# Where the inverse roots of a layer norm are taken, and how many signals TensorE gives per pair

## The reference, cut to what matters

```python
proj = gat_out @ Wp + bp
h = x + jax.nn.elu(proj)
mu = jnp.mean(h, axis=-1, keepdims=True)
var = jnp.mean((h - mu) ** 2, axis=-1, keepdims=True)
out = (h - mu) * jax.lax.rsqrt(var + LN_EPS) * gamma + beta      # first inverse root
...
x = _layernorm(x + out, axis=-1)                                 # second inverse root
```

## Time and profile before

| | us |
|---|---|
| median of three runs | 1848.58 (1843.01 to 1853.82) |
| the profiled execution | 1859.29 |
| its span, first to last instruction | 1857.5 |
| mean granted clock of TensorE | 0.805 |
| TensorE, VectorE, ScalarE, GpSimd busy | 69%, 65%, 47%, 54% |

### The profile page before, as it was taken

The page is one execution under the profiler, slowest core; times in us unless marked ns, Lnnn a source line. Parts: engine busy times, 40 slices in busy tenths (PEclk is TensorE's granted clock), DMA queues, the critical chain, the costliest instruction groups (busy, mean ns, idle before and its releaser), DMA issues. The chain is left out here.

```text
span 1857.5 us, 19719 instructions
## 1 busy us (share of the span) xinstructions
PE 1280.9 (69%) x5229; PEld 791.0 (43%) x5253; DVE 1202.5 (65%) x2284; ACT 876.8 (47%) x1944; POOL 994.5 (54%) x993
## 2 busy tenths in 40 slices
PE   5887787787787782068888887427667666666662
PEld 4555555555555551023444444314343344333331
DVE  4767667667667676857776777318475566665574
ACT  2667667657666673034444443405343344443341
POOL 5655555555555530003555555555676666776665
PEclk9898898888899896579888888558777777777776
DMA  4445545555545542011111111113122222222310
GB/s 114 138 149 170 156 142 169 160 152 163 165 142 162 163 135 95 0 28 30 44 51 46 44 43 44 27 38 69 36 67 50 59 61 62 61 61 50 74 46 22
DMA packets 162058, 161.98 MB, mean 87 GB/s; under 512 B 82994, under 2 KB 99681, under 8 KB 161948
## 3 DMA queue, kind: packets, MB, share of 16 engines
q1 hardware_dynamic: 130300, 130.80, 22.8%
q0 software_dynamic: 31648, 29.92, 7.7%
HBM read 66.88 MB, written 83.27 MB: 81 GB/s over the span
## 5 line engine op out<-in xcount | busy, mean ns | idle before, releaser
L277 POOL DMA_INDIRECT ids_pairs<-in_x_dram,gix x392 | 383.7, 979 | 296.9 <-PE bank L605 149.5
L1208 POOL DMA_INDIRECT x_table<-first_xr,first_rows x200 | 202.3, 1011 | 331.8 <-DVE first_xr L1445 273.3
L1605 POOL DMA_INDIRECT second_raw<-x_table,gix x196 | 201.0, 1026 | 142.7 <-PE twin L1711 60.8
L1611 POOL DMA_INDIRECT out_dram<-second_orow,last_rows x196 | 202.5, 1033 | 70.8 <-issue 58.5
L587 PE MATMUL twin<-AC,dense_hb 128*128 128x256 f32 x784 | 198.1, 397 | 37.7 <-DVE dense_hb L741 25.5
L579 PE MATMUL bank<-dense_xT,Mblk 128*128 128x512 f32 x196 | 125.6, 727 | 71.5 <-ACT dense_rl L670 53.2
L587 PEld LDWEIGHTS twin<-AC,dense_hb 128*128 128x128 f32 x784 | 147.0, 198 | 64.9 <-DVE dense_hb L741 31.4
L749 DVE TENSOR_REDUCE dense_v<-dense_q 128x8 f32<-128x512 f32 x98 | 66.7, 681 | 110.7 <-ACT dense_q L645 108.9
L1245 PE MATMUL twin<-first_zb,Mhead 128*128 128x512 f32 x200 | 129.3, 736 | 0.0
L595 PE MATMUL bank<-prm,dense_xT 128*128 128x128 f32 x784 | 118.5, 300 | 2.4 <-DVE dense_yc L784 2.3
L1385 DVE TENSOR_TENSOR first_zb<-twin,first_df 128x512 f32<-128x512 f32 x100 | 66.6, 686 | 79.0 <-remote 58.8
(11 more groups left out here) (360 smaller groups left out, 3072.5 us busy)
## 6 DMA issues: line engine op xcount, KB each, us to landing
x_table<-dense_yc SPq DMA_DIRECT2D x98, 260.0 KB
ids_rows<-in_x_dram SPq DMA_DIRECT2D x98, 256.0 KB
out_dram<-dense_orow SPq DMA_DIRECT2D x98, 256.0 KB
XT<-dense_turned SPq DMA_DIRECT2D x50, 256.0 KB
target_rows<-first_xr SPq DMA_DIRECT2D x50, 128.0 KB
ids_pairs<-in_x_dram,gix POOLq DMA_INDIRECT x392
second_targets<-target_rows SPq DMA_DIRECT2D x49, 128.0 KB
first_mask<-mask_rows SPq DMA_DIRECT2D x50, 64.0 KB
```

Source lines behind the costliest of these rows:

```text
L277: pool.indirect_dma_start(out=pairs[e % 2][:, j % 4, F * (j // 4):F * (j // 4) + F], out_offset=None, in_=x, in_offset=bass.IndirectOffset ...
L1208: pool.indirect_dma_start(out=x1, out_offset=bass.IndirectOffsetOnAxis(ap=first_rows[:, at + j:at + j + 1], axis=0), in_=xr[b][:, 2 * j + ...
L1605: pool.indirect_dma_start(out=raw[u.off % 3][:, 2 * j + s, :], out_offset=None, in_=x1, in_offset=bass.IndirectOffsetOnAxis(ap=gix[:, at:a ...
L1611: pool.indirect_dma_start(out=out, out_offset=bass.IndirectOffsetOnAxis(ap=last_rows[:, at:at + 1], axis=0), in_=orow[u.off % 4][:, 2 * j ...
```

## The change: what it does

ScalarE's `guess_roots` goes. VectorE adds eps itself (`add_eps` for the first variance, one more instruction in `sum_squares` for the second) and calls `root_step` eight times per slot for pairs u-2 and u-3 together, with `elu` after step 3 and `residual` after step 6. `refine_roots` goes, the roots are positive, and `flag` moves from between `scale` and `add_scaled` of pair u-4 to the end of the slot for pair u-3. TensorE signals `z_used` and `rows_made` only with the last instruction: 1 + 1 in place of 5 + 4, so 9 signals per pair; the waits on them follow. `centre` waits for `add_eps` of the pair before (`v1_made`) in place of ScalarE's guess. At the start `v` and `start` are cleared, and ScalarE's load of its table at the head of the stage goes.

```diff
@@ TensorE
-                    nc.tensor.matmul(pY[b][:, :], Mhead[:, n - 1, :] if n else Mblk[:, :], zb[n][:, :],
-                                     start=(n == 0), stop=(n == H)).then_inc(z_used, 1)
+                    last = nc.tensor.matmul(pY[b][:, :], Mhead[:, n - 1, :] if n else Mblk[:, :], zb[n][:, :],
+                                            start=(n == 0), stop=(n == H))
+                    if n == H:
+                        last.then_inc(z_used, 1)
...
                 def centre(u):
                     pe.wait_ge(h_made, u.count(1))
-                    atleast(pe, root_steps, 4 * u.count(0))
+                    atleast(pe, v1_made, u.count(0))
...
-                    nc.tensor.matmul(pC[:, c], xd[u.off % 4][:, c], Cm, start=True, stop=True).then_inc(rows_made, 1)
+                    last = nc.tensor.matmul(pC[:, c], xd[u.off % 4][:, c], Cm, start=True, stop=True)
+                    if j == 3:
+                        last.then_inc(rows_made, 1)
@@ ScalarE
-                act.add_instruction(mybir.InstLoadActFuncSet(
-                    name=nc.get_next_instruction_name(), engine=mybir.EngineType.Activation, act_func_set_id=EXP_AND_LN))
...
-                def guess_roots(u):
...
-                    if u.back(2).valid(PAIRS + 1):
-                        guess_roots(u.back(2))
@@ VectorE
                 def own_part(u):
...
-                    atleast(dve, z_used, u.count(-1) * (H + 1) + 1)
+                    atleast(dve, z_used, u.count(0))
...
                 def product(u, h):
                     dve.wait_ge(spread_made, u.count(0) * H + (h + 1))
-                    atleast(dve, z_used, u.count(-1) * (H + 1) + (h + 2))
...
+                def add_eps(u):
+                    dve.wait_ge(var_made, u.count(1))
+                    atleast(dve, roots_made, u.count(0))
+                    nc.vector.tensor_scalar(v[:, 0:8], pR[:, 0:8], EPS, None, ALU.add).then_inc(v1_made, 1)
+
                 def sum_squares(u):
                     dve.wait_ge(squared, u.count(1))
-                    atleast(dve, root_steps, 4 * u.count(1))
+                    atleast(dve, v2_made, u.count(0))
                     nc.vector.tensor_reduce(s2[:, :], q2[:, :, :], AX.X, ALU.add).then_inc(s_made, 1)
-
-                def refine_roots(u):
...
+                    dve.wait_ge(s_made, u.count(1))
+                    dve.wait_ge(roots_made, u.count(1))
+                    nc.vector.tensor_scalar(v[:, 8:16], s2[:, :], EPS, None, ALU.add).then_inc(v2_made, 1)
+
+                def root(u, k):
+                    if k == 1:
+                        if u.valid(PAIRS):
+                            dve.wait_ge(v1_made, u.count(1))
+                        atleast(dve, v2_made, u.count(0))
+                    if k == ROOT_STEPS:
+                        atleast(dve, flagged, u.count(-1))
+                        atleast(dve, scaled, u.count(0))
+                    root_step(nc, dve, k, v[:, :], w[:, :], ta[:, :], tb[:, :], root_steps, u.count(0), roots_made)
...
-                                            ALU.subtract).then_inc(yc_made, 1)
+                                            ALU.add).then_inc(yc_made, 1)
...
-                    if u.back(3).valid(PAIRS + 1):
-                        refine_roots(u.back(3))
...
-                    if u.back(4).valid(PAIRS):
-                        flag(u.back(4))
...
-                    if u.back(1).valid(PAIRS):
-                        elu(u.back(1))
-                        residual(u.back(1))
+                    if u.back(2).valid(PAIRS):
+                        add_eps(u.back(2))
+                    for k in range(1, ROOT_STEPS + 1):
+                        if has_roots:
+                            root(u.back(2), k)
+                        if k == 3 and u.back(1).valid(PAIRS):
+                            elu(u.back(1))
+                        if k == 6 and u.back(1).valid(PAIRS):
+                            residual(u.back(1))
+                    if u.back(3).valid(PAIRS):
+                        flag(u.back(3))
```

More of the change, by code:

```diff
@@ L1141, in gnn @@
             s2 = sbp("s2", [128, 8])
-            ve, ln, guess, halved, off, w = (sbp(n, [128, 16]) for n in ("ve", "ln", "guess", "halved", "off", "w"))
+            v, w, ta, tb = (sbp(n, [128, 16]) for n in ("v", "w", "ta", "tb"))
             wf = sbp("wf", [128, 8])
@@ L1149, in gnn @@
             stored = [semp(f"stored{i}") for i in range(4)]
[L1150 to L1154, removed]
+            (spread_made, z_made, z_used, diff_made, crossed, scanned, xd_copied,
+             e_made, g_made, h_made, hc_made, sq_made, var_made, rows_made, v1_made, roots_made, root_steps, scaled,
+             yc_made, squared, s_made, v2_made, xr_made, cleared, flagged) = (semp(n) for n in (
+                 "spread_made", "z_made", "z_used", "diff_made", "crossed", "scanned",
+                 "xd_copied", "e_made", "g_made", "h_made", "hc_made", "sq_made", "var_made", "rows_made",
+                 "v1_made", "roots_made", "root_steps", "scaled", "yc_made", "squared", "s_made", "v2_made", "xr_made",
+                 "cleared", "flagged"))
             block = ph.enter_context(nc.Block())
@@ L1305, in _ @@
             def _(act):
-                act.add_instruction(mybir.InstLoadActFuncSet(
-                    name=nc.get_next_instruction_name(), engine=mybir.EngineType.Activation, act_func_set_id=EXP_AND_LN))
                 def copy_targets(u):
-                    atleast(act, rows_made, u.count(-3) * 4)
+                    atleast(act, rows_made, u.count(-3))
                     nc.scalar.activation(xd[u.off % 4][0:64, :], XT[64:128, columns(u, 0)], ACT.Identity,
@@ L1327, in square @@
                     act.wait_ge(hc_made, u.count(1))
-                    atleast(act, rows_made, u.count(0) * 4)
+                    atleast(act, rows_made, u.count(0))
                     nc.scalar.activation(sq[:, :], pH[:, :], ACT.Square, bias=ncbeta[:, :])
@@ L1388, in scan @@
                     b, half = u.off % 2, slice(64 * s, 64 * s + 64)
-                    dve.wait_ge(z_used, u.count(1) * (H + 1))
+                    dve.wait_ge(z_used, u.count(1))
                     atleast(dve, e_made, u.count(-1))
                     atleast(dve, crossed, u.count(0) * 2 + (1 - s))
-                    nc.vector.tensor_tensor_scan(ys[b][half, ::-1], mask[b][half, ::-1], pY[b][half, ::-1],
-                                                 start[half, :] if u.count(0) or not s else 0.0,
+                    nc.vector.tensor_tensor_scan(ys[b][half, ::-1], mask[b][half, ::-1], pY[b][half, ::-1], start[half, :],
                                                  ALU.mult, ALU.add).then_inc(scanned, 1)
@@ L1457, in slot @@
                     if u.static() and u.count(0) == 0:
+                        nc.vector.memset(v[:, :], 1.0)
                         for b in range(4):
                             nc.vector.memset(xr[b][:, :, F:F + 1], 1.0)
+                        nc.vector.memset(start[:, :], 0.0).then_inc(cleared, 1)
+                        dve.wait_ge(cleared, 1)
+                    has_roots = u.back(2).valid(PAIRS + 1)
                     if u.valid(PAIRS):
```

10 lines of the change are left out of this document (1 added, 9 removed).

## The result

The changed kernel takes 1795.72 us (four runs, 1792.19 to 1799.92), the kernel before took 1845.80 us beside it (four runs, 1836.99 to 1853.82): ratio 0.9724 [0.9687, 0.9760] (in brackets here and below: the 95% interval), 50.1 us less. On other chips the same change makes the kernel 1.3% slower; that is what the experiments are about.

A forecast was written before the change was run, and what follows sets the result against it. VectorE was taken as the bound (10.51 us of an 11.03 us slot), late TensorE signals stretching the mean to 13.95. Pairs 42 us less, 3 us more behind: -39 from 1859.29 gives 1820, median 10.7 lower: 1810 us, range 1797 to 1826.

The forecast's parts named there:

- The steps on VectorE: Small instructions in each slot of stage first: net 1.40 us more work, bounds 0.7 to 2.3, undisturbed slot 11.9 us.
- Nothing covers this: VectorE's added steps lie behind the second scan, where the load hides all but 0.52 us, so they are paid.
- The long waits go: Forecast case, chance 0.43: in the pairs TensorE's late signals mostly stop holding VectorE; 24 slots of 11.9 us, 49 us less.
- Both go the right way: GpSimd's idle between batches becomes 1.7 us and signals per batch fall from 16 to 9, both against late signals.
- The pairs as 24 like slots with an allowance: Pairs of stage first: 24 slots at 12.2 us, with 0.3 us each for slightly late signals, 293 us, 42 us less.
- Behind the last pair: Slots after the last pair: VectorE makes two or three more rounds of 1.4 us, 3 us more.
- the load of the table: ScalarE's load at the head of the stage goes: at most 1 us, at the start.
- Shorter waits, same balance: Rival, 0.26: GpSimd's idle share drains signals, so slots settle at 13.0 to 13.9 us; -22 to 0 us, middle 1836 us.
- The waits stay and VectorE pays: slower: Rival, 0.31: long waits remain in the pairs and VectorE's added steps are paid; +21 us, 1870 us, or 1881 us.
- 10 free slots: In the slower rival (0.31), pairs' slots without long waits or their aftermath pay the added 1.4 us in full: 14 us.
- Signals by the rule: Serialized increments at 26.3 ns: 7 signals fewer give back 0.18 us per pair, 4.6 us in all; not in the forecast sum.

The follow-up runs named there:

- before9: The kernel before with 9 signals of TensorE per pair in place of 16: 1557.23 us, 1.0004 on chip 3; 1854.04 us, 1.0053 on chip 7.
- filler7: The kernel before with seven useless dependent steps of VectorE per slot, 16 signals kept: 1742.47 us, 0.9716 on chip 9; 1575.19 us, 1.0087 on chip 1.
- after16: The changed kernel with 16 signals of TensorE per pair in place of 9: 1754.43 us, 0.9768 on chip 13; 1581.81 us, 1.0160 on chip 3.
- filler4: The kernel before with four useless dependent steps of VectorE per slot, 16 signals kept: 1792.17 us, 0.9975 on chip 13.
- half_scatter: The kernel before without four of the eight scatters of each pair, rows left unwritten: 1752.07 us on chip 7, 1548.71 us on chip 3, one run each.

## Why the prediction was right in its mechanism and short in its size

The direction held, and so did the main line of the mechanism: the long waits go and VectorE pays for its steps. What failed is the size of two terms of the sum, the pairs (293 us forecast, 286.9 us measured) and the stretch behind them (3 us more forecast, 1.7 us less measured). The forecast was 1810 us; 1795.72 us lies 14.3 us under it and 1.3 us under the low end of the range. That low end was drawn in: 24 slots at 0.7 us in place of 1.40 give 1793 us, which the measured time would have met, and redone from the bounds of 0.12 and 0.30 us for ten steps the net is about 0.6 to 2.4 us and not 0.7 to 2.3.

- **The steps on VectorE: right, a little low.** Forecast 1.40 us more work and a slot of 11.9 us, measured 1.55 and 12.06; L147, at 0.34 us where an instruction of 0.17 was taken, is as large as the difference. "Nothing covers this" was right for a slot that runs undisturbed, beyond the 0.52 us that the forecast took off. The net cost against such a slot, 11.9 - 11.03 = 0.87 us, came out at 1.02 us on the quiet chip 3; that 20.8 us over 24 slots is 0.87 us too is chance, since the first four slots paid nothing.
- **The long waits go: right, but for one.** The forecast's sign in the trace was no wait of VectorE for "remote" over 3 us and `own_part` 25 times within 285 to 300 us. It is 1.1 us at most and 286.9 us. ScalarE kept one wait of 10.7 us.
- **What heals them: half right.** "Both go the right way" named the pause and the number of signals. before9 on chip 7 (1.0053 with all waits in place) rules the signals out; filler7 on chip 9 (0.9716) and after16 on chip 13 (0.9768) leave the pause.
- **The pairs as 24 like slots with an allowance: failed, 5.9 us too high.** "I allow 0.3 us per slot for signals that are a little late" made 24 x 12.2 = 293 us. The slots took 286.9 us. The fifth `own_part` of the kernel after splits them:

```profile
846.15 0.69 DVE L1365 SCALAR_TENSOR_TENSOR first_zb<-first_mask,first_xd 128x512 f32<-128x512 bf16 x1
```

  The first four slots, in which the pipeline fills, took 40.0 us, where four at 12.2 are 48.8. They took 40.0 us in the kernel before as well, and the forecast priced them as full ones. The other twenty took 247.0 us, where twenty at 12.2 are 244: the usual slot is 12.06 us and not 11.9, and the one long wait that was left made two of them 14.5 and 14.6 us long, about 5 us together. So the signals that are late did cost something like the 7.2 us allowed for them, in one piece. That 286.9 us is also 24 x 11.9 to within 1 us, the sum without an allowance, is luck: short first slots against longer steps and one wait.
- **Behind the last pair: wrong sign, 4.7 us.** "3 us more" became 1.7 us less. As the price of the added rounds the 3 us were right: on quiet chips that stretch takes 74.5 us in before9 and 77.7 to 78.0 us in after16 and the changed kernel. On the late chip it takes 85.5 us before and 83.8 us after, so some 11 us of lateness stood in it before and some 6 us after. The long waits in it, first before, then after:

```profile
ACT first_ve L1343 <- remote: 10.6, 1, 10.6
```

```profile
ACT XT L1077 <- remote: 8.0, 1, 8.0
```

  I had read the waits only up to the last pair, and so priced the late stretch as if it were undisturbed.
- The two terms make 10.6 us. The stretch up to the first pair took 1.1 us more, where it was to lose the load of the table (1.28 us in the trace of before, at L1306, and not "at most 1 us"). 2.8 us more come from the medians: the forecast started from 1848.58 us, and the runs beside the result gave 1845.80. The 2 us that are left lie between profiled executions and medians, and in rounding.
- **"Shorter waits, same balance" (0.26):** the waits didn't settle at a shorter length. In filler4 on chip 13 they keep their seven times and up to 9.6 us, and in filler7 they are nearly gone. What lies between looks like an edge and not a balance, as far as two points on two chips show. That the rival put its finger on GpSimd was right: half the scatters, no waits. Its own form, that GpSimd's share of the slot decides and not the pause, isn't excluded: a batch of 10.2 us fills 91% of filler4's slot of 11.16 us and 87% of filler7's slot of 11.79 us.
- **"The waits stay and VectorE pays: slower" (0.31):** this is what the change does on a quiet chip, 1.0131 [1.0111, 1.0151], by its very term: the price of the free slots and no waits to win back. Its 10 free slots at 1.4 us were priced too high, since a free slot gives 0.52 us back; it is 1.02 us. That the answer depends on the chip stands in no single profile, so the forecast couldn't know it.
- **Signals by the rule:** before9 gives 1.0004 [0.9992, 1.0016] on chip 3, which leaves at most 1.2 us of gain, and 1.0053 on chip 7. The 4.6 us that I estimated from the Trainium skill ("TensorE: Matmul & The Clock Gate", section "The cost: per-tile semaphore tail", 26.3 ns for each increment on completion) don't show. The measurement decides: seven increments fewer per pair gave back nothing that it can tell. That they lay beside other work is likely, not shown.

No complete kernel that was run beats both. On late chips filler7 (0.972 on chip 9) and the changed kernel (0.970 on chip 7) stand level within their intervals, though not on the same chip; on quiet chips the kernel before is the fastest or level. half_scatter shows what a cheaper scatter could be worth on a late chip, up to 93 us in one run (8 us on a quiet one), without the price of the longer slot; a kernel that makes the same rows with fewer or spread scatters wasn't built.

What stays open: why some chips are late and others not; whether it is the pause in front of a batch or GpSimd's share of the slot that decides (filler4 and filler7 change both at once, and thin out TensorE's work a little too); where between 0.90 and 1.58 us the change lies; and whether GpSimd's issuing or the transfers that it starts hold the signals, and how.

## What to carry to other kernels

When an engine waits for a signal whose instruction the trace shows as long done, look at what a third engine does at that time, and test by useless work or by leaving work out before crediting the edit: here seven multiplications of nothing gained 51 us on one late chip, about what the rewritten roots gained on another. Such a hold can have an edge: on chip 13 a pause of 0.90 us left the time as it was, and one of 1.70 us went with 37 us less. Price the ends of a pipeline by their own rows: its first slots were short and its last stretch held late signals, and neither was in the sum. Time a kernel on more than one chip before you call an edit a gain: this one is 0.970 on one and 1.013 on another.

## What the runs showed of the hardware that was not expected

- The same kernel takes 1557 to 1562 us on four chips and 1791, 1793 and 1845 us on three others, with the busy times of VectorE, ScalarE and GpSimd equal to within 1% over the kernel (windows of before9). The longer times go with waits for TensorE's signals that no recorded event ends: none in twelve traces from the four, some in every trace from the three.
- On the late chips TensorE's signals stay away for up to some 9 us after the recorded end of the matmul while GpSimd issues a batch of eight indirect DMAs with a short pause before it (0.97 us for most of the DMAs, 0.30 us between them). In the kernel before all seven long waits of VectorE fell to the seven batches with a pause of 0.76 to 1.05 us before them, and ended between 1.1 us before and 2.0 us after the end of the batch; with 1.55 us or more in every slot one or none came in each of four traces, with 5.9 us none. The ends of matmuls are modelled in the records, but in the hold of the earlier trace rows TensorE goes on to the first head sum, which waits for VectorE's signal of `own_part` (1030.99 us, 0.69 us long) and starts 0.83 us after its end, 8.4 us before the hold is over:

```profile
1032.51 1.02 PE L1245 MATMUL twin<-first_zb,Mblk 128*128 128x512 f32 x2
```

  So TensorE itself went on; what was late was what it had signalled.
- The first root step, a shift on 128x16 integers, takes 0.34 us where the neighbours take 0.17.
